# Two staging tiles for G in a batched cross-attention kernel, in place of one

## The reference

```python
q = heads(x @ W_q);  k_t = heads(text @ W_k);  v_t = heads(text @ W_v)
probs_t  = softmax(q k_t^T / sqrt(8))
text_out = probs_t @ v_t
qsem  = l2norm(probs_t @ text)            # per head, width 256
fused = q k_ip^T / sqrt(8) + 0.5 * (qsem . l2norm(image tokens))
ip_out = (softmax(fused) * spatial_mask) @ v_ip
out = (text_out + ip_out) @ W_out + b_out + x
```

## Time and profile before

| | |
|---|---|
| time, median of 3 runs (us) | 249.46 (247.46 to 250.62) |
| profiled execution (us) | 248.73 |
| its span, first to last instruction (us) | 246.7 |
| TensorE busy, share of the span | 88% |
| its weight loads | 80% |
| VectorE | 74% |
| ScalarE | 68% |
| GpSimd | 60% |
| mean granted TensorE clock | 0.979 |

### The profile page before, as it was taken

How to read it: one execution, slowest core, us unless ns; L and a number is a source line. 1 busy time by engine, 2 the same in 40 slices (tenths; PEclk the granted TensorE clock), 3 DMA queues, 4 the chain that set the end, 5 groups by cost and what they waited for, 6 DMA issues and landing times.

```text
span 246.7 us, 6905 instructions
## 1 busy us (share of the span) xinstructions
PE 217.4 (88%) x1589; PEld 197.3 (80%) x1589; DVE 181.5 (74%) x1147; ACT 168.1 (68%) x554; POOL 149.2 (60%) x255
## 2 busy tenths in 40 slices
PE   8969639949898997989999999999899999899984
PEld 8858629849888896979798888889797889888873
DVE  4727328568595959778695959596977879599894
ACT  2529247469595949688695969595968779597731
POOL 2241201705949495857769494949585876859780
PEclk9997997989999999999999999999999999999999
DMA  5331451622726354444527363635454453524101
GB/s 145 79 110 41 85 149 30 166 70 56 213 49 180 87 149 116 131 133 96 179 54 210 62 187 83 172 96 149 116 145 120 109 161 70 173 53 141 40 4 40
DMA packets 41580, 27.45 MB, mean 111 GB/s; under 512 B 8513, under 2 KB 39898, under 8 KB 41562
## 3 DMA queue, kind: packets, MB, share of 16 engines
q1 hardware_dynamic: 40922, 26.81, 41.1%
q10 hardware_dynamic: 640, 0.43, 0.7%
HBM read 10.06 MB, written 1.43 MB: 47 GB/s over the span
## 4 chain that ended last, share of the span: by engine, by line
DMA 26%; DVE 25%; PE 23%; issue 9%; ACT 6%; SPq 6%; POOL 3%; DVEq 1%; ACTq 0%; POOLq 0%
DMA main_rhs<-g_stage 26%; DVE junk L721 8%; PE main_ps L961 5%; PE main_ps L963 4%; PE pb L1024 4%; SPq L386 4%; DVE norm L721 3%; PE probsT_ps L943 3%; DVE negmax L786 3%; DVE small L723 3%; ACT k_split L590 2%; DVE oT L778 2%; PE main_ps L878 2%; PE score_ps L997 2%; POOL rnorm L509 1%
## 5 line engine op out<-in xcount | busy, mean ns | idle before, releaser
L620 ACT ACTIVATE probs<-score_ps,negmax 128x124 f32<-128x124 f32 x320 | 92.2, 397 | 1.7 <-DVE negmax L786 1.4
L961 PE MATMUL main_ps<-main_rhs,probsT 124*128 124x137 f32 x320 | 68.6, 296 | 17.0 <-DVE small L723 16.5
L721 DVE CUSTOM_DVE_ANT_0 junk<-main_ps,probs 128x124 f32<-128x124 f32 x320 | 77.8, 281 | 3.8 <-PE main_ps L963 3.7
L961 PEld LDWEIGHTS main_ps<-main_rhs,probsT 124*128 124x128 f32 x320 | 49.6, 193 | 24.1 <-DVE small L723 11.8
L963 PE MATMUL main_ps<-main_rhs,probsT 124*128 124x137 f32 x320 | 64.3, 283 | 0.0
L509 POOL TENSOR_TENSOR rnorm<-clamped,exponent 128x20 f32<-128x20 f32 x15 | 53.1, 3543 | 1.1 <-DVE clamped L706 1.1
L574 ACT ACTIVATE probsT<-probsT_ps 124x512 f32<-124x512 f32 x80 | 50.8, 636 | 3.8 <-PE probsT_ps L943 3.6
L786 DVE TENSOR_REDUCE negmax<-score_ps 128x4 f32<-128x496 f32 x80 | 53.1, 664 | 0.0
L963 PEld LDWEIGHTS main_ps<-main_rhs,probsT 124*128 124x128 f32 x320 | 49.8, 192 | 0.0
L943 PE MATMUL probsT_ps<-ident_sb,probs 128*124 128x128 f32 x320 | 49.3, 278 | 0.0
L943 PEld LDWEIGHTS probsT_ps<-ident_sb,probs 128*124 128x124 f32 x320 | 39.6, 142 | 6.3 <-issue 0.7
(11 more groups left out here) (162 smaller groups left out, 324.1 us busy)
## 6 DMA issues: line engine op xcount, KB each, us to landing
main_rhs<-g_stage SPq DMA_DIRECT2D x16, 660.0 KB, 4.1
vrep<-vip_d SPq DMA_DIRECT2D x13, 320.0 KB, 3.5
k_diag<-k_stack SPq DMA_DIRECT2D x60, 48.0 KB, 2.1
ctxT_sb<-ctxT SPq DMA_DIRECT2D x16, 124.0 KB, 2.7
k_diag<-k_stack SPq DMA_DIRECT2D x60, 32.0 KB, 2.0
xT_sb<-xT SPq DMA_DIRECT2D x16, 80.0 KB, 2.1
xn_sb<-xn SPq DMA_DIRECT2D x15, 80.0 KB, 2.0
out<-out_sb SPq DMA_DIRECT2D x15, 80.0 KB, 3.5
```

Of the source, the lines that this page charges most:

```text
L620: last = act.activation(probs[p][:, h, :], score_ps[(p * G + g) % 2][:, j * TOK:j * TOK + T], ACT.Exp, bias=negmax[p][:, h:h + 1])
L721: dve.tensor_tensor_reduce(junk[:, 2 * r + a, :], u, probs[wb][:, h, :], 1.0, 0.0, ALU.mult, ALU.add, norm2[wb][:, h:h + 1])
L961: pe.matmul(main_ps[r][:, 0:MAIN], probsT[mp][:, 2 * r, :], blk[:, RW - MAIN:RW], start=True, stop=True)
```

## The change

`g_stage` becomes two tiles. Batch b+1 is copied into tile n (n is 1 for odd batches, 0 for even ones), and its replication reads that tile. The wait of ScalarE ahead of the copy is now for the replication of batch b-1, the last that read this tile, in place of that of batch b. Order and number of the instructions stay.

```diff
-        g_stage = sb("g_stage", [TOK, NIP + TOK])
+        g_stage = two(sb, "g_stage", [TOK, NIP + TOK])
...
-                         g_stage[:, :].unsqueeze(1).broadcast_to([TOK, NPAIR, NIP + TOK])).then_inc(s_grep[0], 16)
+                         g_stage[0][:, :].unsqueeze(1).broadcast_to([TOK, NPAIR, NIP + TOK])).then_inc(s_grep[0], 16)
...
                     sp.dma_start(main_rhs[n][:, :, D + 1:D + 1 + NIP + TOK],
-                                 g_stage[:, :].unsqueeze(1).broadcast_to([TOK, NPAIR, NIP + TOK])).then_inc(s_grep[n], 16)
+                                 g_stage[n][:, :].unsqueeze(1).broadcast_to([TOK, NPAIR, NIP + TOK])).then_inc(s_grep[n], 16)
...
                         wait(act, s_ctx_mm, b + 2)
-                        wait(act, s_grep[p], 16 * (i + 1))
-                        act.activation(g_stage[:, NIP:NIP + TOK], pa[:, 0:TOK], ACT.Copy)
-                        act.activation(g_stage[:, 0:NIP], pa[:, T:TOK], ACT.Copy).then_inc(s_gstage, 1)
+                        wait(act, s_grep[n], 16 * (i + p))
+                        act.activation(g_stage[n][:, NIP:NIP + TOK], pa[:, 0:TOK], ACT.Copy)
+                        act.activation(g_stage[n][:, 0:NIP], pa[:, T:TOK], ACT.Copy).then_inc(s_gstage, 1)
```

More of the change, by code:

```diff
@@ L566, in _ @@
             act.wait_ge(s_ctx_mm, 1)
-            act.activation(g_stage[:, NIP:NIP + TOK], pa[:, 0:TOK], ACT.Copy)
-            act.activation(g_stage[:, 0:NIP], pa[:, T:TOK], ACT.Copy).then_inc(s_gstage, 1)
+            act.activation(g_stage[0][:, NIP:NIP + TOK], pa[:, 0:TOK], ACT.Copy)
+            act.activation(g_stage[0][:, 0:NIP], pa[:, T:TOK], ACT.Copy).then_inc(s_gstage, 1)
             def transposed(t, tp):
```

## The result

The changed kernel takes 222.53 us (median of 4, 222.15 to 223.65) against 249.44 us (247.46 to 250.62) in the same runs: 0.8936 of the time, 95% interval 0.887 to 0.9002. The forecast was 225, with a range of 219 to 235. The profiled execution took 222.15 us with a span of 220.2, so 26.5 us of the span are gone. Ratios leave out executions over 1.5% above the fastest of the same kernel, so they can differ from the quotient of two medians.

What follows compares the result with a forecast made beforehand. The prediction took a ring through SyncE's queue and the replication of G to set the 13.30 us window. Gains of 10 us early and 14 us in windows 3 to 14 sum to 24, giving 225 us, range 219 to 235.

Steps and rivals of the forecast that it cites:

- The ring: Steady window: k_stack, SyncE's queue, replication of G, next G copy close a loop of 13.3 us; the change cuts it.
- What the wait held up: Behind ScalarE's G copy: k_split, then VectorE and TensorE; without the wait VectorE starts k_split 1.5 us sooner.
- TensorE next: Steady window: after the wait goes TensorE is the next bound, 11.97 us a window at its own pace.
- the image rows: Rival: their load takes the removed wait's place before the K transposition, ring 12.9 us, 236 to 237 us; chance 0.10.
- less room: Rival: TensorE, busy 12.47 of 13.30 us, has only 0.83 us of idling to win per window; 229 us; chance 0.20.
- more room: Rival: windows shrink to the 11.39 us for which weight loads are busy; 215.5 us; chance 0.03.
- The three stalls: TensorE's stalls in groups 1, 2 and 3 of a steady window, 0.77, 0.18 and 0.38 us, all go.
- The size of a steady window: 11.97 us plus 0.2 for two tight margins (oT, V columns) gives 12.15; bounds 11.97 and 12.65.
- The first windows: Up to window 3's K transposition: 10 us gained, bounds 6 and 11.7, with the image-row queue limiting window 1.
- the ring of 11.1 us: From one K transposition over the replication's issue and the image rows' landing to the next: 6.5 + 4.6 us.
- Slower: Rival: image rows land so late that their ring exceeds 13.42 us; at 14.7 us, 259 us in all; chance 0.03.
- no change: Rival: ScalarE meets another wait at the same place before the G copy; 249 us; chance 0.04.

Runs made afterwards that it cites:

- the GpSimd experiment: One more GpSimd operation of about 0.32 us ahead of the V columns: changed kernel 220.71 us, ratio 0.8889; kernel before 248.56 us, ratio 1.0009.
- the second profile: The changed kernel run once more with nothing edited; ratio against the kernel before 0.8991, measured 221.58 us.

## Why the prediction was right, point by point

- **The ring.** Right, and shown: 46.5 us of waiting and windows of 13.38 us (65.19 to 212.42) come back with the old wait alone, and most of the waiting goes (6.9 us are left) when the replication is issued ahead of k_diag.
- **What the wait held up.** Right in kind. Taking K out from behind it brings half the gain; for the rest the list names Q, which I had not named, and no run shows it.
- **TensorE next.** Right, and shown three times: 0.44 us of added work lengthens the window by 0.44, 0.76 us less shortens it by 0.77 once the image rows are no longer waited for, and before the change the same 0.44 vanished in the stall. The rival "less room", taken from the busy row (12.47), fell: busy time itself shrank to 11.82. The rival "more room", from the weight loads (11.39), fell too; these stayed at 11.29. The measured window lies between them. The Trainium skill's warning ("Perfetto Trace Analysis", Identifying the Most-Contended Engine) that matmul busy time misleads held here: it fell from 12.47 to 11.82 us for the same work.
- **The three stalls.** All three went or nearly so: those of groups 1 and 2 wholly, 0.11 of 0.38 us left in group 3, where I had foreseen VectorE's oT with 0.2 us in hand.
- **The size of a steady window.** The term that was mis-sized: 12.15 us, lower bound 11.97, against 11.84 measured, below the 12.0 to 12.4 us named as the sign of being right. Two parts. The pace was taken from the steps ahead of the mains alone, but the mains of groups 1 and 2 were themselves slower before: in group 1 from their start to the K transposition 0.99 us before (160.67 to 161.66) and 0.84 after (140.75 to 141.59), in group 2 a like 0.14. That is 0.29 us that I had counted as work, and 11.97 - 0.29 + 0.11 = 11.79. From VectorE's timeline and that of the weight loads in the kernel before, group 1:

```profile
160.43 0.18 DVE L723 COPY small<-main_ps 128x26 f32<-128x26 f32 x1
160.94 0.18 DVE L723 COPY small<-main_ps 128x26 f32<-128x26 f32 x1
```

```profile
160.66 0.30 PEld L961 LDWEIGHTS main_ps<-main_rhs,probsT 124*128 124x128 f32 x2 [0.84 <-DVE small L723]
...
161.17 0.30 PEld L961 LDWEIGHTS main_ps<-main_rhs,probsT 124*128 124x128 f32 x2
```

  The weights of the second pair of mains start to load 0.05 us after the end of VectorE's second copy (161.12), as those of the first pair do after the first (160.61). So VectorE held the second pair as well, and the stall I took as one wait was two; what of the 0.29 us is that wait, and what a pipeline that fills again, the rows don't separate. And the 0.2 us for margins rested in half on the V columns, a false reading of which batch they serve, which the GpSimd experiment took away. Together 14.0 us forecast for windows 3 to 14, and 17.4 measured. The start came out smaller than forecast and these windows larger, so the total, 24 us against 26.5, is nearer than its terms by some luck.
- **The first windows.** Right for window 1: the image rows took the removed wait's place there (and for 0.32 us in window 2 of the second profile). The two turns after it were not paced by the ring of 11.1 us, as forecast: no wait for these rows stands in them in the first profile, and they took 12.54 us, with the fall of the clock, and 11.23. The size was 10 us forecast (6 to 11.7) and 8.6 measured. The replication of window 1 was issued at 29.30, not 28.8: SyncE's issues run without a wait from 19.26, 1.1 us sooner than before (20.35), but one of them, the load of x at 22.67, held SyncE for 1.39 us where it took 0.59 before. And the replication took 5.3 us to land, not 4.1. From the transfers, SyncE's timeline and the chain that ended last of the changed kernel, in windows 0 and 1:

```profile
main_rhs<-g_stage SPq DMA_DIRECT2D x1, 660.0 KB, 5.3
```

```profile
19.26 0.56 SPq L344 DMA_DIRECT2D kip_d<-kip_split  x1
...
22.67 1.39 SPq L366 DMA_DIRECT2D xT_sb<-xT  x1
...
29.30 0.67 SPq L392 DMA_DIRECT2D main_rhs<-g_stage  x1
30.07 0.64 SPq L359 DMA_DIRECT2D k_split<-kip_d  x1
```

```profile
30.07 4.73 DMA k_split<-kip_d
```

  So it landed at 34.6 and the image rows at 34.80, and the transposition that waits for them started at 34.94: they came 0.2 us behind the replication that stood before them, where the sum had 0.5.
- **No cost of the tile, no change of the tail.** Right: 0.9935 with the tile alone, and 0.5 us at the tail.
- **Slower, and no change.** Neither happened: in the changed kernel the image rows were waited for in window 1, once more in window 2 of the second profile, and not in the steady windows.

## What to carry to other kernels

When one engine stands for a transfer, follow the ring to where it closes, with the queue that issues the transfer and everything that stands in it, before pricing the wait; the gain is the distance from that ring to the next bound, here 13.4 to 11.84 us, and not the 47.7 us in the list. Take the next bound from start-to-start times in a stretch with no stall at all, since the instructions behind a stall can be slower or stand for a second wait, and before giving a margin to a reader of a double-buffered tile, look which batch it reads. After a wait is gone, look at what is queued behind the transfer that was waited for: here moving a 5 KB load ahead of the 660 KB was worth some 4 us more, the stall and the clock behind it together.

## What the runs showed of the hardware

A stall of TensorE of 2.4 us was followed by a granted clock of 0.60 and 0.54 over the four microseconds from 36 to 40 in one execution of the changed kernel (0.5 is the level of 1.2 GHz, 1.0 that of 2.4), and by 1.00 in another, and in the kernels with G made twice, with half the projections and with the added GpSimd operation, each with a stall of 2.4 us at the same place. In two of these executions it fell elsewhere: the second one of the changed kernel in window 0, and the one with half the projections after a stall of 1.95 us in window 4. The replication of the same 660 KB landed in 4.0 to 4.2 us in the steady windows; of the first ones, one took 5.9 us before the change, and two took 5.3 and 5.8 after it. What makes either difference was not tried.
